# Reordering the opening and the evacuation order of an attention stage

## The reference, cut to what matters

```python
qkv = _bn(_conv(x, qkv_w), qkv_g, qkv_b, qkv_m, qkv_v)      # 1x1 conv, then batch norm
...                                                         # areas: Ba = 16, Na = 1024
attn = jnp.einsum('bhdn,bhdm->bhnm', q, k) * scale
attn = jax.nn.softmax(attn, axis=-1)
out = jnp.einsum('bhdm,bhnm->bhdn', v, attn)
y = out + pe                                                # pe: 7x7 depthwise conv of v
return _bn(_conv(y, proj_w), proj_g, proj_b, proj_m, proj_v)
```

## Time and profile before

| | us |
|---|---|
| three runs of the kernel before | 5036.81, 5043.22, 5051.45; median 5043.22 |
| the profiled execution, its own time | 5046.74 |
| span of that execution, first to last instruction | 5044.6 |
| first score tile of the attention stage (end of the opening) | 181.87 |
| last exponentials' score tile | 2520.0 |

### The profile page before, as it was taken

How to read it: one execution, slowest core, us unless ns; L and a number is a source line. 1 busy time by engine, 2 the same in 40 slices (tenths; PEclk the granted TensorE clock), 3 DMA queues, 4 the chain that set the end, 5 groups by cost and what they waited for, 6 DMA issues and landing times. The chain is left out here.

```text
span 5044.6 us, 78265 instructions
## 1 busy us (share of the span) xinstructions
PE 4255.1 (84%) x20420; PEld 1764.0 (35%) x20420; DVE 3297.5 (65%) x6598; ACT 2376.7 (47%) x4441; POOL 2882.2 (57%) x1680
## 2 busy tenths in 40 slices
PE   1899999999999999999869994868887878788887
PEld 0222222222222222222247742324444444444443
DVE  5666666666666666666400181268888888888887
ACT  0355655555565555566500153324444444444444
POOL 0356665655665655566612221147777777777776
PEclk9799999999999999999989997989999999999999
DMA  4111111111111111111076677969999999999998
GB/s 165 42 39 49 43 37 43 50 48 40 41 52 31 48 50 43 43 43 43 18 293 255 226 293 225 245 235 367 380 373 372 382 372 383 377 373 379 379 379 331
DMA packets 299424, 956.66 MB, mean 190 GB/s; under 512 B 40992, under 2 KB 74400, under 8 KB 282576
## 3 DMA queue, kind: packets, MB, share of 16 engines
q0 software_dynamic: 165888, 604.05, 31.4%
q1 hardware_dynamic: 133200, 348.78, 20.7%
HBM read 797.39 MB, written 104.43 MB: 179 GB/s over the span
## 5 line engine op out<-in xcount | busy, mean ns | idle before, releaser
L529 DVE TENSOR_REDUCE nmx<-mring 128x1 f32<-128x512 f32 x2048 | 1306.0, 678 | 786.5 <-PE mring L628 786.0
L391 POOL TENSOR_TENSOR psum<-pr 128x2048 f32<-128x2048 f32 x256 | 1159.3, 4529 | 885.3 <-ACT pr L489 885.3
L1344 POOL DMA_INDIRECT gat<-gather_table,idc x1152 | 1329.7, 1154 | 433.7 <-issue 347.0
L489 ACT ACTIVATE pr<-ering 128x512 f32<-128x512 f32 x2048 | 1147.7, 597 | 838.5 <-PE ering L648 833.8
L1460 PE MATMUL pac<-smt,wds 128*128 128x512 f32 x2304 | 1099.1, 622 | 25.6 <-ACT smt L1359 25.6
L648 PE MATMUL ering<-qs,ks 98*128 98x512 f16 x2048 | 785.8, 388 | 78.2 <-ACT pr L489 47.6
L628 PE MATMUL mring<-ks,qs 96*128 96x512 f16 x2048 | 785.1, 391 | 49.0 <-DVE nmx L529 47.0
L1359 ACT COPY smt<-ptr 128x512 f32<-128x512 f32 x576 | 335.5, 582 | 845.9 <-PE ptr L1472 845.0
L1412 DVE SCALAR_TENSOR_TENSOR pbb<-gat,wtc,pa 128x256 f32<-128x256 f32 x1152 | 510.9, 479 | 254.3 <-ACT pa L1369 222.5
L1472 PE MATMUL ptr<-cst,sm 128*128 128x128 f32 x2304 | 370.5, 286 | 321.4 <-DVE sm L1426 320.0
L1460 PEld LDWEIGHTS pac<-smt,wds 128*128 128x128 f32 x2304 | 437.5, 200 | 487.3 <-issue 447.3
(11 more groups left out here) (129 smaller groups left out, 2613.8 us busy)
## 6 DMA issues: line engine op xcount, KB each, us to landing
toep<-toe SPq DMA_DIRECT2D x32, 2048.0 KB, 7.5
gather_table<-pix SPq DMA_DIRECT2D x64, 512.0 KB, 8.4
va<-v_pixel_major SPq DMA_DIRECT2D x40, 512.0 KB, 14.0
gat<-gather_table,idc POOLq DMA_INDIRECT x1152, 6.3
xs<-xa SPq DMA_DIRECT2D x16, 1024.0 KB, 4.8
xin<-xa SPq DMA_DIRECT2D x16, 1024.0 KB, 5.9
qs<-qkh SPq DMA_DIRECT2D x256, 64.0 KB, 2.0
ks<-qkh SPq DMA_DIRECT2D x256, 64.0 KB, 2.0
```

The source lines that it names most:

```text
L391: gp.tensor_tensor(psum[:, k % 2, :, :].rearrange("p h n -> p (h n)"), pr[:, m, :, :].rearrange("p h n -> p (h n)"), pr[:, m + 1, :, :].re ...
L489: act.activation(pr[:, step % NT, n % HQ, :], ering[n % 2][:, :], ACT.Exp).then_inc(s_e, 1)
L529: dve.tensor_reduce(nmx[:, g, n // CH, n % CH:n % CH + 1], mring[n % 3][:, :], AX.X, ALU.max, negate=True).then_inc(s_mf, 1)
L1344: gp.indirect_dma_start(gat[:, r, :, :].rearrange("p q c -> p (q c)"), None, tab, bass.IndirectOffsetOnAxis(ap=idc[:, e, u:u + 1], axis=0) ...
```

## The change

In the opening the constant rows of `ks` are set by GpSimd, behind the normalisation of area 0 and ahead of its splits. TensorE waits at first for the weights alone (`s_w`); it waits for `s_ready` and the constant rows only before slot 0. It makes the four projection tiles of group 0, then the max units, with the four tiles of group 1 put behind units 32, 36, 40 and 44. Each stacking of area 0 is halved: SP issues the DMAs of two heads, ScalarE those of the other two.

In the slots, the projection tiles move to slots 10, 12, 14 and 16, and ScalarE evacuates each in the slot after: `qkf` between the two exponentials, `qkh` behind the second (and behind `copy_num`, where the slot has one). VectorE does the first max chunk of a slot, then the value tile, then the other chunks.

```diff
-            QK_AT = (NT + 3, NT + 11)
+            QK_TILES = tuple(range(NT + 2, NT + 9, 2))
+            QK_SLOTS = tuple(n + 1 for n in QK_TILES)
...
+            def stack_rows(eng, j, odd, g, heads):
+                for dst, r, src, t in ((qs2, 0, qkh, 0), (ks2, 0, qkh, 1), (qs2, 2, qkh, 0), (ks2, 1, qkh, 1),
+                                       (qs2, 1, qkl, 0), (ks2, 2, qkl, 1)):
+                    if src is qkl:
+                        eng.wait_ge(s_hl, j * 4 + (2 * g + t + 1))
+                    for h in heads:
+                        eng.dma_start(dst[HD * r:HD * r + HD, odd, g, h, :], src[HD * h:HD * h + HD, t, :]
+                                      ).then_inc(s_stk[g], 16)
...
-                    stack(0, 0, 0)
-                    stack(0, 0, 1)
+                    for g in range(HG):
+                        stack(0, 0, g, range(HQ // 2))
...
                     normalise(0)
+                    gp.memset(ks2[96:98, :, :, :, :], MS).then_inc(s_ksz, 1)
+                    gp.wait_ge(s_ksz, 1)
+                    gp.sem_inc(s_gate, 1)
...
                                     act.activation(pr[:, step % NT, n % HQ, :], ering[n % 2][:, :],
                                                    ACT.Exp).then_inc(s_e, 1)
+                                    if x == 0 and not last and slot in QK_SLOTS:
+                                        qk_evac(i + 1, g, QK_SLOTS.index(slot), 0)
                                 if slot == NUM_SLOT[0]:
                                     copy_num(i, g, 0)
...
-                                if not last:
-                                    for n in share(slot, *QK_AT, QKN):
-                                        qk_evac(i + 1, g, n)
+                                if not last and slot in QK_SLOTS:
+                                    qk_evac(i + 1, g, QK_SLOTS.index(slot), 1)
 
                     for g in range(HG):
                         for n in range(QKN):
-                            qk_evac(0, g, n)
+                            for part in range(2):
+                                qk_evac(0, g, n, part)
+                        act.wait_ge(s_qke, qcount(0, g, QKN))
+                        stack_rows(act, 0, 0, g, range(HQ // 2, HQ))
...
-                    ch.did(dve.memset(ks2[96:98, :, :, :, :], MS))
...
-                                    for n in share(slot, 0, M_END, MXN):
+                                    mx = share(slot, 0, M_END, MXN)
+                                    for n in mx[:1]:
                                         max_chunk(i + g, 1 - g, n)
...
+                                if not (g and last):
+                                    for n in mx[1:]:
+                                        max_chunk(i + g, 1 - g, n)
...
-                    pe.wait_ge(s_ready, 2)
+                    pe.wait_ge(s_w, 48)
...
-                                if not last:
-                                    for n in share(slot, *QK_AT, QKN):
-                                        qk_tile(i + 1, g, n)
+                                if not last and slot in QK_TILES:
+                                    qk_tile(i + 1, g, QK_TILES.index(slot))
...
-                    for g in range(HG):
-                        for n in range(QKN):
-                            qk_tile(0, g, n)
+                    for n in range(QKN):
+                        qk_tile(0, 0, n)
                     for n in range(MXN):
                         max_unit(0, 0, 0, n)
+                        if n >= MXN // 2 and n % 4 == 0 and n // 4 - MXN // 8 < QKN:
+                            qk_tile(0, 1, n // 4 - MXN // 8)
                     max_transpose(0, 0, False)
+                    pe.wait_ge(s_ready, 2)
+                    pe.wait_ge(s_ksz, 1)
```

More of the change, by code:

```diff
@@ L236, in build @@
             s_w = sem("s_w")
-            s_ready = sem("s_setup_done")
+            s_ready, s_ksz = sem("s_setup_done"), sem("s_shift_rows")
             s_xin, s_cur, s_xn = sem("s_xin"), sem("s_cur"), sem("s_xn")
@@ L309, in load_x, with stack @@
                         sp.dma_start(xin[:, :, :], src.rearrange("a p k n -> p (a k) n")).then_inc(s_xin, 16)
-                    def stack(j, odd, g):
+                    def stack(j, odd, g, heads=range(HQ)):
                         sp.wait_ge(s_qke, qcount(j, g, QKN))
[L314 to L320, removed]
+                        stack_rows(sp, j, odd, g, heads)
                     def max_rows(j, odd, g):
@@ L443, in _, with qk_evac @@
                     act.activation(vsc, vrow[:, 3, :], ACT.Sqrt).then_inc(s_vs, 1)
-                    def qk_evac(j, g, n):
+                    def qk_evac(j, g, n, part):
                         t, c = n // CH, n % CH
[L447 to L451, removed]
+                        if part == 0:
+                            act.wait_ge(s_qk, j * (2 * QKN) + (g * QKN + n + 1))
+                            if n == 0 and (g or not isinstance(j, int) or j):
+                                act.wait_ge(s_hl, j * 4 + 2 * g)
+                                act.wait_ge(s_stk[1 - g], j * STK + g * STK)
                         col = (QB, KB)[t] + g
[L453 to L456, removed]
+                        act.activation((qkf, qkh)[part][:, t, c * 512:(c + 1) * 512], wbank[:, :],
+                                       ACT.Identity, bias=bsh[:, col:col + 1], scale=bsc[:, col:col + 1]
+                                       ).then_inc(s_qke, 1)
                     def copy_num(i, g, c):
@@ L556, in body @@
                                 if not (g and last):
-                                    for n in share(slot, 0, M_END, MXN):
+                                    mx = share(slot, 0, M_END, MXN)
+                                    for n in mx[:1]:
                                         max_chunk(i + g, 1 - g, n)
[L559 to L562, removed]
+                                else:
+                                    mx = ()
                                 if g == 0:
@@ L572, in body @@
                                                           ).then_inc(s_ve, 1)
+                                if not (g and last):
+                                    for n in mx[1:]:
+                                        max_chunk(i + g, 1 - g, n)
+                                    if slot == M_END - 1:
+                                        max_all(i + g, 1 - g)
+                                    if slot == M_END + 1:
+                                        max_parts(i + g, 1 - g)
                                 if 0 < slot - DEN_SLOT[0] <= RP:
```

## The result

The changed kernel takes 4930.9 us (median of four runs, 4926.03 to 4932.91), the kernel before 5045.85 in the runs beside it: a ratio of 0.9772, 95% interval 0.9755 to 0.9789. Beside the later experiments the kernel before had medians of 5036 to 5042, so this one is the highest of them. I forecast 4960, with a range from 4935 to 5005. The profiled execution took 4926.03, its span is 4924.2.

What follows compares the result with a forecast made beforehand. TensorE's own instruction list was taken as the bound, so only its waits could be won. Opening 24, value tile 56 and slots 3 sum to 83: 4964 from the profiled 5046.7, 4960 against the median, range 4935 to 5005.

Steps and rivals of the forecast that it cites:

- The opening: Stretch before the first score tile: the first score would come 24 us earlier (5 to 32).
- The value tile: Attention slots: TensorE would no longer wait for the value tile's evacuation on VectorE, gaining 56 us (40 to 60).
- The slots: Projection tiles moved to slots 10 to 16: net 3 us gained (20 gained to 25 lost).
- slot 11's wait: Late max unit in slot 11: 15 us saved in group 1; in group 0 GpSimd's normalisation wait replaces it, loss 2.
- the 0.16 waits: Slots 14, 16 and 20: waits of 0.16 for an exponential behind a pair of evacuations would go, 14 us.
- the evacuations between exponentials: Odd slots: the second exponential comes 0.78 later, close to even for TensorE, taken as 0 (up to 0.2 each).
- the copy in slot 17: The second evacuation behind slot 17's copy would make slot 19's score wait 0.8, costing 24 us in all.
- The value waits: Rivals on TensorE's waits for value tiles: back in part, 4988, chance 0.12; back in full, 5016, chance 0.07.
- the evacuations do not pace the scores: Denies the rival that ScalarE's evacuations in slots 11 to 17 delay scores by 174 us, 5134; chance 0.09.
- neither the memset nor ScalarE's issue: Denies the rival that GpSimd's 34 us memset or doubled ScalarE issue time loses 8 to 15, 4970 to 4977; chance 0.10.
- the second queue: Stacking before the first score: two queues would save 7.6 us; rival that they are no faster, 4968, chance 0.05.
- The wait for maxima: Sign in the changed kernel's profile: TensorE's total wait for maxima would be down by some 12 us.

## Why the prediction was right or wrong

- **The opening, 24 forecast, 25 measured.** The steps came out: first tile 10.3 earlier (10.6), stacking 7.3 shorter (7.6), the maxima 12 us closer to the landing, 6.0 of stalls among them (6). They make 23.5; the rest is luck. Ahead of the stacking, the kernel before had a second slow tile, which the changed kernel's profile doesn't have; other profiles of the same opening have two or three slow ones:

```profile
98.06 3.78 PE L604 MATMUL wbank<-xn,wqk 128*128 128x512 f32 x4 [1.54 <-ACT qkh L454]
```

  The stalls came out although one reading behind them was wrong. I took the 3.75 of the tile at 92.77 for a tile at the lower clock, but the granted clock (third figure from the end) was 1.00 there:

```profile
92.00:100.00 8.00, 5.69 (x7) 2.08 (x8) 0.57 (x2) 1.45 (x2) 0.00 (x0) 1.00 0.00 0
```

  Among the maxima of the changed kernel it did go as I said: the first tile took 3.62 at 0.50, the next ones 1.98 at 1.00. The memset took 13.75 us where I had 16.8, and was hidden as argued. Two costs were missed: SP's queue ahead of the row DMAs and ScalarE's square root ahead of the evacuations. The change avoids both, so they did not show.
- **The value tile, 56 forecast, 67.5 measured: the step that failed, by its size.** The mechanism held in every pass. But I took the waits' idle time with 0.16 each for the tail of the instruction before, 60, and then shaved 4 for waits that might stay. None stayed, and there is a third piece: a value tile that had to wait also runs longer itself. The groups of TensorE within the attention, before and after (count, busy us, mean ns, idle us before):

```profile
L615 PE MATMUL wbank<-wvs,xn 128*128 128x256 f32 x512 | 141.5, 400 | 50.0 <-DVE vt L570 50.0
```

```profile
L632 PE MATMUL wbank<-wvs,xn 128*128 128x256 f32 x512 | 132.7, 381 | 0.0
```

  50.0 of idle time, 65 x 0.16 = 10.4, and 6.8 of the 8.8 us by which the busy time fell make 67.2, against 67.5 in the slots whose tiles had waited. The other 2 of busy time lie in the tiles of slot 1, which did not wait. The 1.13 of the earlier trace rows beside the 1.03 of an unhindered tile would have told me.
- **The slots, 3 forecast, 11 measured, the second term that was too small.** Group 0's exchange of slot 11's wait for GpSimd's, the 0.16 waits, the evacuations between exponentials (no cost) and the copy in slot 17 went as argued, 0.7 to 0.8 of loss there. In group 1 I counted one late max unit, 1.0; slots 10 and 11 gave 1.12 in slot 11 and took a tile of 1.72 for 1.48 in slot 10, 1.36 in all. That is 5 of the 8 us missing, and the copy's loss, nearer 0.7 than 0.8 in 30 passes, is another 3.
- **The parts don't quite add.** Alone, the opening gives 25, VectorE's order 78 and the slots 11 in the attention's profiles; together they give 104. Of what VectorE's order wins alone, 5 us in group 0's slots 10 and 11 are lost to GpSimd's wait once the tile stands there; about 5 more are the turns of the loop, which differ between the profiles.
- **The range.** The 104 of opening and attention are 21 more than my 83: 12 from the value tile, 8 from the slots, 1 from the opening. The profiled execution of before, 5046.7, less the 104 is 4943, inside the range; the 16 us behind the attention took it to 4926. So the two terms brought the time to the edge of the range, and chance took it over. The range left no room for what equal code varies there, and it was narrower than my own bounds: 32, 60 and 20 add up to 112, which gives 4931.
- **The rivals.** The value waits came back neither in part nor in full; the evacuations do not pace the scores; neither the memset nor ScalarE's issue, 0.63 as on SP, held up the opening (8 to 15 lost would have been 4968 to 4975, not 4970 to 4977); the second queue saves its issue time. That DMAs of two queues land one behind another was my own addition to the rule cited there.
- **The signs.** The wait for maxima fell by 21.9 and not by 12, as slot 11's wait went in group 0 too, where GpSimd's took its place. The 69 us of group 1's pass were only the length of the window in the earlier trace rows: from first score to first score, where no turn of the loop follows, it takes 67.7 us, and 66.6 after the change. Group 0's fell from 77.7 to 73.8.

## What to carry to other kernels

Where the engine that sets the pace waits, its idle time can be less than the wait costs, here 50.0 of 67.5 us: add the tail of the instruction before it and what the delayed instruction itself loses, or take start to start against a place where the same sequence runs free. In a schedule of slots, an instruction moved to an earlier slot must be checked against every producer that counts from a fixed slot, and one that covered another engine's late work leaves that uncovered: both new waits here were readable beforehand, and a move of one line each took 21 and 23 us off. When a change touches one stage of a long kernel, compare that stage; here the others varied by 20 us with the same code, about what one such move is worth.

## What the runs showed of the hardware that was not expected

- GpSimd's memset of 2 x 16384 16-bit elements takes 13.75 us, as VectorE's does (13.71): 0.84 ns for an element on either.
- The first projection tiles after TensorE's idle time take 3.78 us once, twice or three times ahead of the first of 1.98, with the same instructions; the first score of kernels with one opening came at 156.8, 156.9, 158.4 and 160.7. The granted clock reads 1.00 while such a slow tile runs (82.50 to 86.28 in the changed kernel); why it is slow is not shown:

```profile
81.00:86.50 5.50, 3.78 (x4) 1.18 (x4) 2.30 (x4) 0.18 (x1) 5.35 (x3) 1.00 0.00 0
```

- VectorE's operations on two operands, 0.42 us each, took 1.30 while GpSimd normalised, and GpSimd's pair of operations 2.67 instead of 2.36. The timeline of the changed kernel:

```profile
79.56 0.42 DVE L530 TENSOR_TENSOR num<-yo,vsh 128x256 f32<-128x256 f32 x1
79.72 2.67 POOL L384 TENSOR_SCALAR xn<-xin,cur 128x1024 f32<-128x1024 f32 x2 [8.86 <-DMA xin<-xa]
80.02 1.30 DVE L531 TENSOR_TENSOR yo<-yo,num 128x256 f32<-128x256 f32 x1
81.36 1.30 DVE L532 TENSOR_TENSOR vsh<-yo 128x256 f32<-128x256 f32 x1
```

The Trainium skill, page "SBUF — State Buffer", section "Who interferes with whom", has it that a VectorE instruction with two operands from SBUF contends with a GpSimd instruction that reads SBUF; the rows agree, both engines' work got longer. Here VectorE's had time.
